# Self attention in a decoder layer: heads as units, masks added by VectorE, split probabilities and values

## The reference

```
h = rmsnorm(layernorm(x)) * norm_w
q, k, v = 16 heads of 64 from h @ w_q, h @ w_k, h @ w_v
ll = q k^T / 8, causal within the 512 tokens
idx = the 128 tokens with the highest score h @ scorer_w + b
lg = q k[idx]^T / 8, masked to idx <= position
attn = softmax(concat(ll, lg))
o = attn[..., :512] v + attn[..., 512:] v[idx]
x = x + layernorm(x) + o @ w_out
```

## Time and profile before

| | |
|---|---|
| median of 3 runs | 2303.1 us (2300.76 to 2306.99) |
| the profiled execution | 2303.6 us, span 2301.9 us |
| PE busy | 2120.8 us, 92% of the span |
| DVE busy | 1320.5 us, 57% |
| ACT busy | 930.6 us, 40% |
| POOL busy | 343.7 us, 15% |
| mean granted TensorE clock | 0.945 of full speed |

### The profile page before, as it was taken

One profiled execution on the slowest core, in us unless ns is written; L12 is line 12 of the kernel. 1 busy time (PEld: TensorE's weight loads), 2 busy tenths in 40 slices (PEclk: granted clock), 3 DMA queues, 4 the chain that ended last, 5 costly groups with the idle time before them and its releaser, 6 DMA issues. The chain is left out here.

```text
span 2301.9 us, 36078 instructions
## 1 busy us (share of the span) xinstructions
PE 2120.8 (92%) x12029; PEld 1654.5 (72%) x12029; DVE 1320.5 (57%) x3145; ACT 930.6 (40%) x1989; POOL 343.7 (15%) x605
## 2 busy tenths in 40 slices
PE   3999999999999999999999999996899999978899
PEld 2886787688588688778868868864788888854543
DVE  5584376178167347537717826743787878745401
ACT  3442344244144244334415414424866666413210
POOL 2100100010010010001001001003554445320000
PEclk9999999999999999999999999996987878769899
DMA  5000000100100100000010010002013212150000
GB/s 192 1 2 33 24 1 13 44 1 1 56 1 1 55 3 1 27 31 1 11 47 1 1 57 1 1 33 81 27 59 133 61 58 67 51 201 1 1 0 19
DMA packets 46137, 80.24 MB, mean 35 GB/s; under 512 B 10067, under 2 KB 10067, under 8 KB 45448
## 3 DMA queue, kind: packets, MB, share of 16 engines
q1 hardware_dynamic: 45320, 75.85, 9.9%
q0 software_dynamic: 640, 2.10, 0.2%
HBM read 60.11 MB, written 17.83 MB: 34 GB/s over the span
## 5 line engine op out<-in xcount | busy, mean ns | idle before, releaser
L403 ACT ACTIVATE probs<-s_bank,nmax 128x512 f32<-128x512 f32 (+3 forms) x512 | 249.5, 526 | 368.5 <-DVE nmax L534 266.4
L686 PE MATMUL o_bank<-vals,probs_t 128*128 128x65 f32 x2560 | 329.0, 272 | 0.1
L686 PEld LDWEIGHTS o_bank<-vals,probs_t 128*128 128x128 f32 x2560 | 312.5, 192 | 13.1 <-DVE probs_t L542 12.9
L534 DVE TENSOR_REDUCE nmax<-s_bank 128x1 f32<-128x512 f32 (+2 forms) x384 | 184.4, 508 | 189.2 <-PE s_bank L663 186.5
L710 PE MATMUL pj_bank<-w_o,o_t 128*128 128x512 f32 x512 | 221.8, 594 | 6.0 <-ACT o_t L411 6.0
L542 DVE COPY probs_t<-pt_bank 128x512 f32<-128x512 f32 x320 | 217.8, 681 | 2.2 <-PE pt_bank L671 2.1
L671 PE MATMUL pt_bank<-ident,probs 128*128 128x128 f32 x1280 | 194.9, 275 | 15.7 <-DVE o_t L449 15.7
L659 PE MATMUL s_bank<-k_twice,q_both 128*128 128x512 f32 (+3 forms) x512 | 190.0, 373 | 2.1 <-DVE k_lo L522 2.1
L710 PEld LDWEIGHTS pj_bank<-w_o,o_t 128*128 128x128 f32 x512 | 96.6, 190 | 126.5 <-issue 126.5
L381 ACT ACTIVATE vals<-pj_bank,twice 128x512 f32<-128x512 f32 x64 | 43.9, 688 | 340.4 <-PE pj_bank L583 334.8
L518 DVE SCALAR_TENSOR_TENSOR q_both<-pj_bank,q_both 64x512 fp32r<-64x512 f32 x128 | 88.1, 688 | 141.7 <-ACT q_both L390 139.1
(11 more groups left out here) (268 smaller groups left out, 4125.3 us busy)
## 6 DMA issues: line engine op xcount, KB each, us to landing
xb<-in_x SPq DMA_DIRECT2D x9, 1024.0 KB, 5.8
xt<-x SPq DMA_DIRECT2D x36, 256.0 KB, 2.8
probs<-in_x SPq DMA_DIRECT2D x32, 256.0 KB, 2.6
x<-probs SPq DMA_DIRECT2D x32, 256.0 KB, 2.0
am<-in_L_ffn_attention_mask SPq DMA_DIRECT2D x8, 1024.0 KB, 5.3
out<-x SPq DMA_DIRECT2D x32, 256.0 KB, 2.5
w_sb<-in_L_ffn_w SPq DMA_DIRECT2D x2, 4096.0 KB, 20.4
o_t<-in_L_attn_w_v SPq DMA_DIRECT2D x2, 1024.0 KB, 9.6
```

The source lines that it names most:

```text
L403: ins = nc.scalar.activation(probs[:, i % 2, c0:c0 + nk], s_bank[i % 2][:, c0:c0 + nk], ACT.Exp, bias=nmax[:, i % 4, n:n + 1])
L534: ins = nc.vector.tensor_reduce(nmax[:, i % 4, n:n + 1], s_bank[i % 2][:, c0:c0 + nk], AX.X, ALU.max, negate=True)
L686: ins = nc.tensor.matmul(o_bank[slot][:, o0:o0 + VW], probs_t[:, i % 2, c0 + P * kt:c0 + P * kt + P], vals[:, kt, 2 * p + h, :], start=(kt ...
```

## The change

- A head has three units (`unit_rows`): the last 128 query rows with 512 keys; the first and third 128 rows with 128 and 384 keys; the second with 256. There are 48 units a batch, and `probs` has four slots.
- The mask matmul is gone. VectorE adds a mask to the scores while it reads them out of PSUM and takes the row minimum in the same instruction (q is scaled by -1/8, so the sign is turned). The masks hold the causal part and, for a chosen key, -ln 2, which doubles its exp; they are built once a batch from a transposed row (`tw`, `build_masks`).
- ScalarE's exp works in place on `probs` and sums the row (`den`). VectorE inverts it, GpSimd multiplies the probabilities (`r`).
- `t` stands three units after `s` and has 4, 4 or 2 transposes. ScalarE writes the high part of what was turned (`turned_hi`), VectorE the low part (`turned_lo`), four units after.
- `pv` is made once a head: `vals` holds high and low parts side by side as the stationary operand, and the turned probabilities move past it, 512, 128, 384 and 256 columns, first high and then low: eight matmuls. The output stands with features on partitions, so no later transpose is needed; ScalarE copies one half, VectorE adds the other (`o`).
- q and k weights are split at the start and stored in DRAM (`w_pairs`); each pair's weights are loaded again for each batch. Their projections run in thirds of four matmuls between units; high and low parts are written in one step (`q_split`, `k_split`). The next batch's first pair is projected at the end of a batch.

```diff
-UNITS = 5
+UNITS = 3
+RING = 4
-RANK_AT = (22, 24, 27, 29)
+RANK_AT = (28, 31, 34, 37)
+HT_AT = 41
+def unit_rows(u):
+    return ([(3, 0, 512)], [(0, 0, 128), (2, 128, 384)], [(1, 0, 256)])[u]
 def attention_plan():
+    thirds = {}
+    for i in range(1, NPAIR + 1):
+        q0 = UNITS * 2 * (i - 1) - 2 if i < NPAIR else NU - 1
+        for j in range(3):
+            thirds[q0 + j] = ("q" if j == 2 else "q_part", i if j == 2 else 2 * i + j)
+            thirds[q0 + 3 + j] = ("k" if j == 2 else "k_part", i if j == 2 else 2 * i + j)
+    for g in range(-2, NU + 6):
+        if 0 <= g - 1 < NU:
+            plan.append(("r", g - 1))
+        if 0 <= g - 4 < NU:
+            plan.append(("turned_hi", g - 4))
+        if 0 <= g < NU:
             plan.append(("s", g))
+        if 0 <= g - 4 < NU:
+            plan.append(("turned_lo", g - 4))
+        if g >= 8 and (g - 8) % UNITS == 0 and (g - 8) // UNITS < NH:
+            plan.append(("o", (g - 8) // UNITS))
+        if g - 1 in thirds and thirds[g - 1][0] in ("q", "k"):
+            plan.append((thirds[g - 1][0] + "_split", thirds[g - 1][1]))
+        if 0 <= g - 3 < NU:
+            plan.append(("t", g - 3))
+        if g >= 7 and (g - 7) % UNITS == 0 and (g - 7) // UNITS < NH:
+            plan.append(("pv", (g - 7) // UNITS))
+        if g in thirds:
+            plan.append(thirds[g])
...
 sync:
+            for i in range(3):
+                load_weights(i)
+            store_parts(0)
+            load_weights(3)
+            store_parts(1)
...
+            def load_pairs(b, pairs):
+                for p in pairs:
+                    sp.wait_ge(k_low_ready, b * NPAIR + p - 1)
+                    load_pair(p % NPAIR)
 gpsimd:
+                    if kind == "r":
+                        pl.wait_ge(den_ready, b * NU + i + 1)
+                        for n, (_, c0, nk) in enumerate(unit_rows(i % UNITS)):
+                            part = probs[:, i % RING, c0:c0 + nk]
+                            ins = nc.gpsimd.tensor_tensor(part, part, rden[:, i % 4, n:n + 1].broadcast_to((P, nk)),
+                                                          ALU.mult)
 scalar:
+            def q_high(b, i):
+                act.wait_ge(pj_ready, ready)
+                for h in range(2):
+                    ins = nc.scalar.activation(q_both[own, i % 2, h, :], pj_bank[slot][own, :], ACT.Copy,
+                                               scale=-HD ** -0.5)
+                ins.then_inc(q_hi_ready, 1)
...
             act.wait_ge(split_lo, len(W_ORDER))
+            act.wait_ge(w_stored[1], STORED[5])
             with act.Fori(0, B) as b:
...
                     if kind == "s":
                         act.wait_ge(max_ready, b * NU + i + 1)
+                            ins = nc.scalar.activation(part, part, ACT.Exp, bias=nmax[:, i % 4, n:n + 1], scale=-1.0,
+                                                       accum_out=den[:, i % 4, n:n + 1])
                         ins.then_inc(p_ready, 1)
...
 vector:
                     if kind == "s":
                         dv.wait_ge(s_ready, b * NU + i + 1)
+                        nc.vector.memset(carrier[:, 6 + i % 4:7 + i % 4], 0.0)
+                            ins = nc.vector.tensor_tensor_reduce(
+                                probs[:, i % RING, c0:c0 + nk], s_bank[i % 2][:, c0:c0 + nk],
+                                masks[:, m0 + c0:m0 + c0 + nk], 1.0, 3e38, ALU.add, ALU.min, nmax[:, i % 4, n:n + 1])
                         ins.then_inc(max_ready, 1)
+                    if kind == "r":
+                        dv.wait_ge(p_ready, b * NU + i + 1)
+                        nc.vector.reciprocal(rden[:, i % 4, 0:n], den[:, i % 4, 0:n]).then_inc(den_ready, 1)
+                    if kind == "turned_lo":
+                        dv.wait_ge(hi_ready, b * NU + i + 1)
...
+                    if kind == "o":
+                        dv.wait_ge(ob_ready, b * NH + i + 1)
+                        nc.vector.tensor_tensor(o_t[rows, i // 2, :], o_bank[i % 2][0:HD, :], o_b[rows, :],
+                                                ALU.add).then_inc(o_ready, 1)
 tensor:
                     if kind == "s":
                         if i >= 2:
-                            pe.wait_ge(p_ready, b * NU + i - 1)
+                            pe.wait_ge(max_ready, b * NU + i - 1)
-                            ins = nc.tensor.matmul(s_bank[slot][:, c0 + nk - P:c0 + nk], ident_b[:, :], causal_b[:, :],
-                                                   start=False, stop=True)
...
+                        parts = [(p, k) for p in (p_hi, p_lo) for k in (0, 3, 1, 2)]
+                        for n, (part, k) in enumerate(parts):
+                            ins = nc.tensor.matmul(o_bank[i % 2][:, 0:P * (TT - k)], vals[:, k, i, :],
+                                                   part[:, i % 2, KEYS_AT[k], :], start=(n == 0),
+                                                   stop=(n == len(parts) - 1))
```

More of the change, by code:

```diff
@@ L281, in _ @@
             sp.dma_start(xb[:, :, :], x_rows[0]).then_inc(x_in, 16)
+            load_pairs(B - 1, range(2, NPAIR + 1))
             results(B - 1)
@@ L371, in _ @@
                         normed(None, 0, c)
+                if i == 3:
+                    act.wait_ge(w_stored[0], STORED[0])
+                    q_high(None, 0)
+                    k_high(None, 0)
             act.wait_ge(split_lo, len(W_ORDER))
+            act.wait_ge(w_stored[1], STORED[5])
             with act.Fori(0, B) as b:
@@ L464, in rank, with build_masks @@
                     step(nc.vector.tensor_tensor(cnt[:, 0, :], cnt[:, 0, :], cnt[:, 1, :], ALU.add))
-                    if b is not None:
-                        dv.wait_ge(v_ready, n * (2 * TT))
-                    nc.vector.tensor_scalar(twice[:, :], cnt[:, 0, :], TOPK - 0.5, 1.0, ALU.is_lt,
-                                            ALU.add).then_inc(twice_ready, 1)
+                    nc.vector.tensor_scalar(chosen[:, :], cnt[:, 0, :], TOPK - 0.5, -LN2, ALU.is_lt,
+                                            ALU.mult).then_inc(chosen_ready, 1)
+            def build_masks(b):
+                slot, ready = pt(b, ("tw", 0))
+                dv.wait_ge(pt_ready, ready)
+                row = pt_bank[slot]
+                for at, n in ((0, 3), (640, 2), (1024, 1)):
+                    done.mark(nc.vector.tensor_copy(masks[:, at:at + P * n], row[:, 0:P * n]))
+                for at, k in ((384, 3), (512, 0), (896, 2), (1152, 1)):
+                    ins = nc.vector.tensor_tensor(masks[:, at:at + P], row[:, P * k:P * k + P], later_keys[:, :], ALU.add)
+                done.wait(dv)
+                ins.then_inc(masks_ready, 1)
             def normed(b, n, c):
@@ L497, in _ @@
             split(2)
+            split(3)
+            q_low(None, 0)
+            k_lows(None, 0)
             score_row(None, 0)
-            split(3)
+            split(4)
             for t in range(TT):
                 rank(None, 0, t)
-                if t in (1, 3):
-                    split(4 + t // 2)
-            with dv.Fori(0, B) as b, done.loop(b, 2 * TT + 2 * TT + 1 + NU, B):
+                if t == 1:
+                    split(5)
+            with dv.Fori(0, B) as b, done.loop(b, TT + TT + 2 * TT + 1 + 3, B):
@@ L610, in transposed, with rows_of, score_rows, project @@
                 ins.then_inc(pt_ready, 1)
-            def score_rows(b, n):
-                slot, _ = pt(b, ("score", 0))
-                pe.wait_ge(score_ready, n + 1)
-                pt_empty(b, ("score", 0))
+            def rows_of(b, key, columns):
+                slot, _ = pt(b, key)
+                pt_empty(b, key)
                 for t in range(TT):
                     ins = nc.tensor.transpose(pt_bank[slot][:, P * t:P * t + P],
-                                              score[:, t:t + 1].broadcast_to((P, P)), ident[:, :])
+                                              columns[:, t:t + 1].broadcast_to((P, P)), ident[:, :])
                 ins.then_inc(pt_ready, 1)
+            def score_rows(b, n):
+                pe.wait_ge(score_ready, n + 1)
+                rows_of(b, ("score", 0), score)
+            def project(b, kind, i, thirds):
+                slot, _ = pj(b, (kind, i))
+                hi, lo = (w_qk[:, i % 2, 2 * (kind == "k") + k] for k in range(2))
+                for n in range(4 * thirds[0], 4 * thirds[-1] + 4):
+                    c, form = divmod(n, 3)
+                    w, moving = ((hi, ht_hi), (lo, ht_hi), (hi, ht_lo))[form]
+                    ins = nc.tensor.matmul(pj_bank[slot][:, :], w[:, c, :], moving[:, c, :], start=(n == 0),
+                                           stop=(n == 3 * DC - 1))
+                if thirds[-1] == 2:
+                    ins.then_inc(pj_ready, 1)
             pe.wait_ge(const_made, N_CONST)
@@ L623, in _ @@
                 transposed(None, 0, c)
+            pe.wait_ge(ht_lo_ready, DC)
+            pe.wait_ge(split_lo, 1)
```

(3 more changed lines are left out.)

447 lines of the change are left out of this document (238 added, 209 removed).

## The result

The changed kernel takes 2762.5 us (median of four, 2761.75 to 2764.37) against 2301.9 (2300.01 to 2306.99): 1.200 times as long, 95% interval 1.198 to 1.202. The forecast was 2645, the range 2540 to 2790. The profiled execution has a span of 2761.3 us, 459.4 more than before.

A forecast was written before the change was run, and what follows sets the result against it. TensorE bounds the kernel before; afterwards the VectorE-ScalarE loop would. A batch goes from 188.5 to 226.6 us, eight times giving +305, plus 37 at the start and 1.7 around the 2301.9 span: 2645 us, range 2540 to 2790.

The forecast's parts named there:

- What sets the time: In the units, VectorE and ScalarE, both in order, wait for each other each step; 19.66 us per split pair; chance 0.69.
- One of the signs I had named: In the units, TensorE's scores would wait for VectorE's minimum if the forecast was right; no size given.
- TensorE's pair of 13.5 us: TensorE's work per pair of heads falls from 16.4 us to 13.5, within 13.5 to 14.8.
- Prices of the loop: Instruction and handover times added unit by unit along VectorE and ScalarE: 19.66 us per split pair, 13.32 without splits.
- Values and output: Projection stretches of a batch: values 24.4 us, output projection unchanged at 28.5 us.
- The rest of the batch: Units 148.3 us, next batch's scorer 12, normalised rows 4.4, last unit to first output matmul 9.
- the term of 12 us: VectorE's statistics, dot, score and ranking for the next batch stand mostly uncovered in the loop: 12 us a batch.
- the turned rows: Next batch's normalised rows: four low parts of 0.75 us and two uncovered high parts of 0.69, 4.4 us a batch.
- GpSimd's division: In the units, GpSimd's 3.1 us a head beside 9.8 us is covered by three units of lag.
- The start: Before the first batch, ScalarE waits until split q and k weights lie in DRAM, near 87 us: +37 us.
- The rival of the clock: In the units, TensorE's clock falls to 0.65, its pair takes 20.8 us; 2707 us in all; chance 0.17.
- The rival that TensorE stays the bound: In self attention, TensorE's sum still sets the time, 165 us a batch, about 2153 us in all; chance 0.07.

The follow-up runs named there:

- the loop open: Changed kernel with VectorE's reciprocal behind the next minimum, and its q/k low parts and o sum one unit behind ScalarE's steps; 2479.8 us.
- the last version: Changed kernel reordered, turned rows through projection banks, next batch's scorer work beside value and output projections, ScalarE's stored-weights wait moved later; 2250.4 us.
- the closed loop: Changed kernel's own VectorE/ScalarE order; there, statistics, dot and score moved beside the value projections and ranks into the first pair measured 2627.9 us.

## Why the prediction was right, and where its terms were not

- **What sets the time: right.** VectorE and ScalarE alternate, as the two timelines show, and opening the order gives 283 us back. One of the signs I had named hardly came: TensorE's scores wait for the minimum in only 8 units (14.1 us); what they wait for is k's low part.
- **TensorE's pair of 13.5 us: right.** With the loop open it is busy for 13.25 of 14.4 us. Five such pairs of the last version stand at 14.5 to 14.8 us. The 16 products of the change cost 2.7 us a pair (eight from 626.61 to 627.96), between the bounds of 2.25 and 3.6.
- **Prices of the loop: the sum right, in part by luck.** A clean pair takes 19.3 us, forecast 19.66, but two terms missed in opposite directions: ScalarE's row sum costs about 0.1 us, and the step from VectorE to ScalarE, forecast 0.12 us, takes 0.03 (625.67 + 0.08 to 625.78). The new instructions, by form (count, busy us, mean ns, idle before):

```profile
L674 DVE CUSTOM_DVE_ANT_0 probs<-s_bank,masks 128x512 f32<-128x512 f32 x128 | 87.5, 684 | 0.0
L674 DVE DVE_READ_ACCUMULATOR2_ANT nmax<- 128x1 f32 x512 | 42.3, 83 | 0.0
L501 ACT ACTIVATION_READ_ACCUMULATOR probs<-probs,nmax 128x1 f32 x512 | 95.6, 187 | 0.0
L428 POOL TENSOR_TENSOR probs<-probs,rden 128x512 f32<-128x512 f32 x128 | 133.1, 1040 | 459.7 <-DVE rden L681 459.7
```

  The minimum with mask is the nearest row of before: 684 ns. ScalarE's row sum is a read of 187 ns of its own, which begins 0.09 us before its exp ends (625.78 + 0.72 against 626.41): about 0.1 us net where an exp is followed by its reader, where I let it cancel. Exp on 128 columns takes 402 ns here from SBUF, 368 before from PSUM: 34 ns more. The Trainium skill (VectorE: DVE Perf Modes, section The TRN2 errata) gives an estimate of 43 for that; the rows lie between it and the 22 I had taken.
- **Values and output: right.** 24.2 against 24.4, 28.8 against 28.5.
- **The rest of the batch: undersized.** Units with the stretch to the output took 190.3 us on average (243.3 less 24.2 and 28.8), where 148.3 + 12 + 4.4 + 9 = 173.7 were forecast. The step that failed is the term of 12 us for VectorE's work for the next batch's scorer: I added its busy time to the loop and no more. It cost some 23 us (moved away in the closed loop, 16.8 came back and the ranks still cost 6.1 in the first pair). The dot did cost its own 3 us (a pair of 22.2, against 19.3), but the statistics and the score with its rank cost 6 each: there TensorE's transposes wait behind the extra work, TensorE comes back at half clock, and the next scores are late. How much of the 11 us of excess is the clock and how much the waits was not taken apart. For the turned rows I put 4.4; the run that moved them to other banks gave 11.3 (in the opened loop), so that term was too small as well. The remaining few us I did not divide.
- **GpSimd's division "three units of lag cover it": right in a clean pair**, wrong in the pair with the statistics. I had not asked what stands ahead of it in GpSimd's order; the run without it gave 4.4 us there.
- **The start: oversized.** Forecast +37, measured +17.3. TensorE's third value projection starts at 66.40 us, had 49.67. I took a DMA rate from one 4 MB load, about 200 GB/s, and waited for all 17 MB. The first 69 us of the profile show 277 GB/s, and what ScalarE waits for is the stores of the split weights (ScalarE's timeline, then TensorE's). That wait is only the last link: with it moved away TensorE's projection came 3.2 us earlier, and VectorE's ranking steps held it.

```profile
65.03 1.07 ACT L491 CAST vals<-pj_bank 128x512 fp32r<-128x512 f32 x2 [9.78 <-DMA w_pairs<-p_lo]
66.40 0.79 PE L717 MATMUL pj_bank<-wv_hi,ht_hi 128*128 128x512 f32 x1 [18.58 <-DVE vals L654]
```

- **The untouched blocks: +4.3 us**, which I did not follow up.
- **The rival of the clock: half right, in places I had not named.** In clean pairs the clock is 0.95 and TensorE doesn't join. In the pairs with scorer work it does (0.77). That the range held is partly luck: its high end was made of row sums (87 us) and the clock (62), while the excess came with the scorer's work and the turned rows, and no run measured the clock's share of it. The sum of the misses: 8 x 16.6 - 19.7 + 4.3 = 117 us, which is 2762 - 2645.
- **The rival that TensorE stays the bound** gave 2153 us, with 165 us a batch. Its sum was near: in the batch of the last version shown above TensorE is busy for 162.5 of 178.8 us, and 13.8 of the 16.3 without work lie in the units. Order brought the same work from 2762 to 2250 us; why the rest stays was not followed up.

## What to carry to other kernels

When a step's two halves lie on two engines that take their work in order, put the second half one step of the list later; compare the order of instructions, not the busy shares, which were under 60% on both engines that set the time here. Side work put into such a loop can cost more than its own time (some 23 us for 12 here), since what it delays on a third engine comes back as a late input; put it in a stretch where that engine has nothing to do. Before a change is given up for being slower, ask whether its work or its order did it: here the order of the same work, with two changes of banks and scratch and one wait moved, was worth 512 of 2762 us.

## What the runs showed of the hardware

- An exp that also sums its row is two instructions on ScalarE, and the second, a read of one value, takes 187 ns, more than twice the 83 ns of VectorE's.
- GpSimd multiplies 512 columns by one value a row in 1040 ns, 128 in 399 ns; with an operand as wide as the tile, 616 columns took 1491.
- Behind waits of 1.68 and 4.51 us (rows above) TensorE ran at half clock: four transposes 1.09 and 1.11 us, against 0.61 in the earlier trace rows. Not every wait did that: behind one of 2.24 us in the clean pair (for k's low part, to 632.70 us) the granted clock was 1.00 and the next four transposes took 0.63. With the loop open, its waits in a clean pair were 0.29 to 0.42 us and its clock 1.00.
- 6.29 us passed on VectorE between the last instruction of its loop and the first of the next round, the last 4.3 of them with its input there and no wait in the trace that ended them.
